# Who fetches which chunk in a three-round graph kernel: SP takes every third unit, ScalarE also works in round one

## The reference

```
ew = (w - min w) / (max w - min w + 1e-8)
h  = relu(layernorm(x))
for each edge:  m = ew * (h[src] @ W1[type]);   h1 = relu(segment_sum(m, dst) + h @ root1 + b1)
for each edge:  m = ew * (h1[src] @ W2[type]);  x  = x + segment_sum(m, dst) + h1 @ root2 + b2
h   = relu(layernorm(x))
out = x + segment_sum(w * h[src], dst) @ W3.T + b3
```

## Time and profile before

| | us |
|---|---|
| median of 3 runs | 5746.92 (5746.85 to 5749.39) |
| profiled execution, its own time | 5746.24 |
| its span | 5744.4 |
| POOL busy | 4320.2 (75%) |
| PE busy | 3123.5 (54%) |
| DVE busy | 1414.0 (25%) |
| ScalarE busy | 439.1 (8%) |

### The profile page before, as it was taken

One profiled execution on the slowest core, in us unless ns is written; L12 is line 12 of the kernel. 1 busy time (PEld: TensorE's weight loads), 2 busy tenths in 40 slices (PEclk: granted clock), 3 DMA queues, 4 the chain that ended last, 5 costly groups with the idle time before them and its releaser, 6 DMA issues.

```text
span 5744.4 us, 66657 instructions
## 1 busy us (share of the span) xinstructions
PE 3123.5 (54%) x11399; PEld 2517.6 (44%) x11399; DVE 1414.0 (25%) x5042; ACT 439.1 (8%) x1183; POOL 4320.2 (75%) x4580
## 2 busy tenths in 40 slices
PE   3766666666666544444444444444444444444444
PEld 3645555545545434434434434434444444444444
DVE  7433333333333222122222222221111111111111
ACT  5111111111111000000000000000000000000000
POOL 7777777777777677777777777777777777777777
PEclk7887877887778655555555555555555555555555
DMA  6222222222222222222222222222222222222222
GB/s 174 82 76 74 72 74 76 72 74 76 72 74 75 63 63 62 61 62 62 61 62 62 62 61 62 62 60 61 62 62 60 62 62 61 62 62 62 61 62 59
DMA packets 291274, 392.97 MB, mean 68 GB/s; under 512 B 94699, under 2 KB 205144, under 8 KB 290840
## 3 DMA queue, kind: packets, MB, share of 16 engines
q0 software_dynamic: 146304, 299.92, 20.0%
q1 hardware_dynamic: 132760, 85.71, 5.0%
q10 hardware_dynamic: 11776, 3.04, 0.2%
HBM read 336.96 MB, written 51.34 MB: 68 GB/s over the span
## 4 chain that ended last, share of the span: by engine, by line
POOL 68%; issue 23%; ACTq 3%; DMA 2%; PE 2%; DVE 1%; ACT 1%; SPq 0%; DVEq 0%; POOLq 0%
POOL rows L558 68%; ACTq L798 2%; DMA rows<-table,idx 2%; ACTq L793 1%; PE bank L975 1%; PE bank L1016 1%; DMA spare_a<-table 0%; ACT acc L628 0%; PE bank L893 0%; PE bank L915 0%; DVE acc L1223 0%; DVE bank L1372 0%; DVE stats L1094 0%; SPq L359 0%; DVE win L1342 0%
## 5 line engine op out<-in xcount | busy, mean ns | idle before, releaser
L558 POOL DMA_INDIRECT rows<-table,idx x4508 | 4254.7, 944 | 1394.8 <-issue 1364.2
L1016 PE MATMUL bank<-win,rows 128*128 128x48 f32 x6064 | 1768.6, 423 | 1837.5 <-DMA rows<-table,idx 1821.9
L1016 PEld LDWEIGHTS bank<-win,rows 128*128 128x128 f32 x6064 | 1458.6, 319 | 2148.1 <-DMA rows<-table,idx 2128.2
L975 PE MATMUL bank<-win,rows 128*128 128x192 f32 x3080 | 856.6, 408 | 638.0 <-DMA rows<-table,idx 493.7
L975 PEld LDWEIGHTS bank<-win,rows 128*128 128x128 f32 x3080 | 596.7, 229 | 849.4 <-DMA rows<-table,idx 672.4
L1223 DVE TENSOR_TENSOR acc<-acc,bank 128x48 f32 x1173 | 239.3, 204 | 1111.2 <-PE bank L893 960.7
L1342 DVE TENSOR_SCALAR win<-iota,key,sw_col 128x192 f32<-128x192 f32 x1563 | 501.4, 391 | 15.9 <-PE bank L908 13.2
L688 ACT ACTIVATE tile_T<-acc 128x128 f32<-128x128 f32 x196 | 60.4, 309 | 2411.2 <-DVE acc L1223 2411.2
L1285 DVE TENSOR_SCALAR idx<-src_col 128x16 int32<-128x16 int32 x98 | 21.6, 223 | 884.8 <-PE bank L1016 884.8
L893 PE MATMUL bank<-sums,W1s 128*128 128x192 f32 (+1 forms) x784 | 219.3, 446 | 0.6 <-ACT sums L736 0.6
L1372 DVE TENSOR_TENSOR bank<-bank,rel 128x384 f32<-128x384 f32 x392 | 218.6, 558 | 0.7 <-issue 0.2
(11 more groups left out here) (123 smaller groups left out, 1311.9 us busy)
## 6 DMA issues: line engine op xcount, KB each, us to landing
spare<-table SPq DMA_DIRECT2D x9088, 0.5 KB
spare_a<-table ACTq DMA_DIRECT2D x5888, 0.5 KB
rows<-table,idx POOLq DMA_INDIRECT x4508, 2.6
table<-st SPq DMA_DIRECT2D x146, 256.0 KB, 2.3
x_rows<-table SPq DMA_DIRECT2D x49, 128.0 KB
x_rows<-in_x_dram SPq DMA_DIRECT2D x48, 128.0 KB
h_rows<-table SPq DMA_DIRECT2D x48, 128.0 KB
out_dram<-st SPq DMA_DIRECT2D x48, 128.0 KB, 2.1
```

The source lines that it names most:

```text
L558: eng.indirect_dma_start(out=rows[:, slot, :], out_offset=None, in_=table[:, :], in_offset=bass.IndirectOffsetOnAxis(ap=idx[:, slot:slot + ...
L975: ins = eng.matmul(half_ps[v % 2 * 2 + h][:, q % 2 * RW:(q % 2 + 1) * RW], chunk_rows(0, u, q * CG + k), wide[:, v % 2, q * CG + k, :], st ...
L1016: ins = eng.matmul(agg_of(u, v, q)[:, q * W:(q + 1) * W], chunk_rows(r, u, q * CG + k), window[:, slot, :], start=(k == 0), stop=(k == n - 1))
```

## The change

`SE` becomes 3: SP fetches chunk 12 of units 5, 8, ... 95 in round 0 and of 2, 5, ... 95 in rounds 1 and 2. A chunk's eight blocks are spread over three passes, as two, three and three. ScalarE fetches chunk 8 (`AK`), the first of a unit's third group, in place of chunk 12, in units 5, 9, ... 93 of rounds 1 and 2 as before, and now also in units 13, 17, ... 93 of round 0 (`AF` = 3: from its fourth on). In round 0 it issues one block at q = 1 and one at q = 3 of each unit, the second ahead of `prep`. A unit can now have both. Another address list is computed on DVE, semaphores are split by round, and one semaphore is dropped from the setup.

```diff
-SE = 4
+SE = 3
 AE = 4
+AF = (3, 1, 1)
...
-    SK = UC - CG
+    SK, AK = UC - CG, UC - 2 * CG
...
-        def by_sp(r, u):
-
-            return u % SE == SE - 1 and (r > 0 or u >= SE)
...
-        def by_act(r, u):
-
-            return r > 0 and u % AE == 1 and AE < u < AO * AE
...
+        def by_sp(r, u, k):
+
+            return k == SK and u % SE == SE - 1 and (r > 0 or u >= RING) and u < NO * SE
+
+        def by_act(r, u, k):
+
+            return k == AK and u % AE == 1 and AF[r] <= u // AE < AO
...
                 else:
-                    j, part = divmod(u + 2, SE)
+                    j, part = divmod(u + 1, SE)
                     if 0 < j < NO:
-                        single_rows(r, j, part * P // SE, (part + 1) * P // SE)
+                        lo, hi = (p * (P // OB) // SE * OB for p in (part, part + 1))
+                        single_rows(r, j, lo, hi)
...
-                    if not is_single(r, u, k):
+                    if not fetched(r, u, k):
                         gather(table, v * UC + k, rows_signal(u, k))
...
+            def act_rows(r, u, lo, hi):
+
+                j, part = divmod(u + AE - 1, AE)
+                if not AF[r] <= j < AO:
+                    return
+                n, b = act_number(r, j), act_buffer(r, j * AE + 1)
+                if part == 0 and lo == 0:
+                    if j == AF[r]:
+                        eng.wait_ge(s_single_at, 8)
+                        for s in range(2):
+                            if r == 0:
+                                eng.wait_ge(s_tabled[s], TABLED[s])
+                            else:
+                                eng.wait_ge(s_stored[s], stored_by(r, s, 0))
...
+                table = in_bytes[r]
+                for e in range(part * P // AE + lo, part * P // AE + hi, OB):
...
                         if q == 2 and u == 1:
                             clear_early()
+                        if q % 2 == 1:
+                            act_rows(0, u, q // 2 * OB, (q // 2 + 1) * OB)
                         if q == UG - 1 and not first(u, 2):
                             eng.wait_ge(s_acc, u * UG)
                             prep(0, u - 2, v % 2)
...
-                    act_rows(r, u)
+                    act_rows(r, u, 0, P // AE)
...
+            eng.tensor_scalar(act_at[0][:, :], act_src[:, :], float(row_bytes), None, ALU.mult).then_inc(s_single_at, 1)
```

More of the change, by code:

```diff
@@ L92, in build @@
         act_src, act_type = sb("act_src", [AO, P], i32), sb("act_type", [AO, P], i32)
-        act_at = [sb(f"act_at{r}", [AO, P], i32) for r in range(2)]
+        act_at = [sb(f"act_at{r}", [AO, P], i32) for r in range(3)]
         single_at = [sb(f"single_at{r}", [NO, P], i32) for r in range(3)]
@@ L138, in build @@
         match_ps = bank[6][:, 64:64 + HC * W].rearrange("p (c w) -> p c w", w=W)
-        s_first, s_first_f, s_first_t = sem("s_first"), sem("s_first_f"), sem("s_first_t")
+        s_first, s_first_t = sem("s_first"), sem("s_first_t")
         s_list = [sem(f"s_list{k}") for k in range(4)]
@@ L163, in build @@
         s_single_list = sem("s_single_list")
-        s_by_act = [sem(f"s_by_act{b}") for b in range(2)]
+        s_by_act = [[sem(f"s_by_act{a}{b}") for b in range(2)] for a in range(2)]
         s_idx_part, s_agg_part = sem("s_idx_part"), sem("s_agg_part")
@@ L231, in rows_signal, with fetched, act_number, act_buffer @@
             return s_tail[k] if u == NU - 1 else s_row[u % RING * UG + k // CG][min(k % CG, CG - 2)]
-        def by_sp(r, u):
-            return u % SE == SE - 1 and (r > 0 or u >= SE)
-        def is_single(r, u, k=SK):
-            return k == SK and (by_sp(r, u) or by_act(r, u))
-        def by_act(r, u):
-            return r > 0 and u % AE == 1 and AE < u < AO * AE
-        def act_number(r, u):
-            return (r - 1) * (AO - 1) + u // AE - 1
+        def by_sp(r, u, k):
+            return k == SK and u % SE == SE - 1 and (r > 0 or u >= RING) and u < NO * SE
+        def by_act(r, u, k):
+            return k == AK and u % AE == 1 and AF[r] <= u // AE < AO
+        def fetched(r, u, k):
+            return by_sp(r, u, k) or by_act(r, u, k)
+        def act_number(r, j):
+            return (0, 0, AO - AF[1])[r] + j - AF[r]
+        def act_buffer(r, u):
+            return ((AO - AF[0] if r else 0) + act_number(r, u // AE)) % 2
         def single_number(r, j):
@@ L255, in single_buffer, with gathers_so_far @@
             return spare[:, n % 2, :]
-        def single_gathers(r, u):
+        def gathers_so_far(r, u, k):
             units_so_far = [(p, w) for p in range(r + 1) for w in range(u % RING, NU - 1 if p < r else u + 1, RING)]
-            return 16 * sum(not is_single(p, w) for p, w in units_so_far)
+            return 16 * sum(not fetched(p, w, k) for p, w in units_so_far)
         def wait_rows(eng, r, u, k):
@@ L265, in wait_rows @@
                 eng.wait_ge(s_tail[k], 16 * (r + 1))
[L266 to L269, removed]
+            elif by_act(r, u, k):
+                eng.wait_ge(s_by_act[r > 0][act_buffer(r, u)], 16 * P * (act_number(r, u // AE) // 2 + 1))
+            elif by_sp(r, u, k):
                 n = single_number(r, u // SE)
@@ L272, in wait_rows @@
                 eng.wait_ge(s_single[r][n % 2], 16 * P * so_far)
-            elif k == SK:
-                eng.wait_ge(rows_signal(u, k), single_gathers(r, u))
+            elif k in (SK, AK):
+                eng.wait_ge(rows_signal(u, k), gathers_so_far(r, u, k))
             elif k % CG < CG - 1:
@@ L281, in chunk_rows @@
         def chunk_rows(r, u, k):
-            if is_single(r, u, k) and by_act(r, u):
-                return spare_a[:, act_number(r, u) % 2, :]
-            if is_single(r, u, k):
+            if by_act(r, u, k):
+                return spare_a[:, act_buffer(r, u), :]
+            if by_sp(r, u, k):
                 return single_buffer(single_number(r, u // SE))
@@ L411, in _ @@
             for to, arr in ((act_src, src), (act_type, etype)):
-                eng.dma_start(to[:, :], arr[0:AO * AE * UC * P].rearrange("(j c e) -> j c e", c=AE * UC, e=P)[:, UC + SK, :]
+                eng.dma_start(to[:, :], arr[0:AO * AE * UC * P].rearrange("(j c e) -> j c e", c=AE * UC, e=P)[:, UC + AK, :]
                               ).then_inc(s_single_list, 16)
@@ L485, in single_rows @@
                     if n == 0:
-                        eng.wait_ge(s_single_at, 7)
+                        eng.wait_ge(s_single_at, 8)
                     elif n > 1:
@@ L730, in finish1_last @@
                     normalise(st[:, h, k * 2 * D:k * 2 * D + D], fin_of(t + k, k)[:, 0:D], 0, k).then_inc(s_fin_a, 1)
+            def act_rows(r, u, lo, hi):
[5 more added lines that the diff above has]
+                    if j == AF[r]:
+                        eng.wait_ge(s_single_at, 8)
+                        for s in range(2):
[3 more added lines that the diff above has]
+                                eng.wait_ge(s_stored[s], stored_by(r, s, 0))
+                    before = [(p, i) for p in range(r + 1) for i in range(AF[p], AO if p < r else j)]
+                    if len(before) > 1:
+                        p, i = before[-2]
+                        if p == 0:
+                            eng.wait_ge(s_half, 2 * (i * AE + 1) + 2)
+                        else:
+                            eng.wait_ge(s_agg, (p - 1) * NU + i * AE + 2)
+                table = in_bytes[r]
+                for e in range(part * P // AE + lo, part * P // AE + hi, OB):
+                    found = nc.values_load_multi_w_load_instructions(
+                        act_at[r][j:j + 1, e:e + OB], engines=(mybir.EngineType.Activation,), min_val=0,
+                        max_val=table.shape[1] - row_bytes,
+                        skip_runtime_bounds_check_because="the lists name nodes of the graph alone")[1]
+                    for k in range(OB):
+                        eng.dma_start(spare_a[e + k:e + k + 1, b, :].bitcast(mybir.dt.uint8),
+                                      table[0:1, bass.ds(found[k], row_bytes)]).then_inc(s_by_act[r > 0][b], 16)
             def first_round():
@@ L775, in first_round @@
                     own_out(t)
[L777 to L799, removed]
             def fast(r):
@@ L850, in _ @@
             eng.wait_ge(s_const, 2)
-            eng.wait_ge(s_first_f, 1)
+            eng.wait_ge(s_first, 17)
             eng.transpose(first_ps[:, 0:P], first_f, ident[:, :]).then_inc(s_first_t, 1)
@@ L1079, in _ @@
             eng.wait_ge(s_first, 16)
-            eng.tensor_copy(first_f, first_f.bitcast(i32)).then_inc(s_first_f, 1)
+            eng.tensor_copy(first_f, first_f.bitcast(i32)).then_inc(s_first, 1)
             link(eng.memset(row0[:, :], 0.0))
@@ L1196, in _ @@
             eng.tensor_scalar(single_at[1][:, :], single_type[:, :], float(row_bytes), None, ALU.mult).then_inc(s_single_at, 1)
[L1197 to L1201, removed]
```

(6 more changed lines are left out.)

## The result

The changed kernel takes 5823.32 us as the median of 4 runs (5822.8 to 5824.81), beside 5746.89 for the kernel before in the same comparison: a ratio of 1.0132, 95% interval 1.0119 to 1.0145. Forecast were 5786 us, 5730 to 5835. The profiled execution took 5822.86 us, its span 5820.9.

What follows compares the result with a forecast made beforehand. POOL's gathers, at a pitch of 1.248 us, were taken as the bound. 5746.2 - 56.2 (gathers saved) + 39.9 (SP's late start) + 56 (ScalarE's late rows) = 5786 us, 8-in-10 range 5730 to 5835.

Steps and rivals of the forecast that it cites:

- Gathers: POOL's table-row gathers, all rounds: 45 fewer at a pitch of 1.248 us, saving 56.2 us.
- SP at the start of round one: SP's late first chunks hold POOL at unit 12 until 290.0 us: one stall of 39.9 us.
- SP later: SP's chunks after its late start, through rounds two and three: no cost, with some 5 us of cover in later rounds.
- ScalarE in round one: ScalarE's two blocks per unit in 84 units delay prep and PE, but cost POOL nothing.
- ScalarE in rounds two and three: ScalarE's late rows, moved to chunk 8, hold POOL: 14 us in round two, 42 in three, 56 us together.
- The forecast's upper bound: For ScalarE's stalls in rounds two and three: 1 us more each, 100 us instead of 56.
- The sum by it, 5809: With 2.0 us fixed DMA cost instead of 1.51, ScalarE's 46 stalls grow up to 0.5 us each, 23 us: 5809.
- A: Rival: only SP's late start costs, ScalarE's moved chunk lands in time: 5730 us, chance 0.10.
- B: Rival: POOL is held neither by SP's late start nor by ScalarE's moved chunk: 5690 us, chance 0.04.
- C: Rival: ScalarE's stalls come but SP's at unit 12 don't: 5746 us, chance 0.04.
- D: Rival: ScalarE's blocks in round one hold PE beyond the cover, 84 units by 1 us: 5870 us, chance 0.07.
- E: Rival: SP, at 97%, falls behind by 1 us in three units, over 27 chunks: 5813 us, chance 0.08.

Runs made afterwards that it cites:

- E2: Changed kernel, but SP's chunks of units 5 and 8 of round one stay with POOL, SP beginning at unit 11: 5786.72 us, ratio 1.0071.
- E6: Changed kernel without ScalarE's chunks in round one: 9109.98 us at a slower pace of issue, ratio 1.144 to the kernel before beside it.
- E1: Changed kernel with ScalarE's four quarters of a chunk issued one unit earlier: 5732.21 us, ratio 0.9973 to the kernel before.
- E4: Changed kernel with places swapped, SP fetching chunk 8 and ScalarE chunk 12: 5737.17 us, ratio 0.9982 to the kernel before.
- E5: Changed kernel with SP's part undone (one chunk every fourth unit, as before), ScalarE's part kept: 5762.75 us, ratio 1.0027 to the kernel before.
- E7: Changed kernel with SP's chunks of rounds two and three left to POOL: 8164.65 us at a slower pace of issue, ratio 1.025; repeated, 1.024.
- E3: Changed kernel, ScalarE's quarters a unit earlier and SP starting at unit 11: 8964.83 us at a slower pace, ratio 1.126; last repetition 8980.14 us.

## Why the prediction came out as it did

**Gathers.** 4463 on table rows and a pitch of 1.248 us: as forecast.

**SP at the start of round one.** As forecast, nearly to the microsecond: unit 11's last row issued at 285.8 (287.6 forecast, with a release at 131.0, not 133.0), POOL held until 288.1 (290.0), 38.6 us in two gaps (39.9), and E2 takes them away. I had not worked out the first gap's share. It is 30 us because PE begins unit 11's third group late too: it stood for unit 8's chunk until 229.93, and then 4.87 and 4.37 us for ScalarE's `prep` at the end of units 9 and 10, in which ScalarE already issues rows. These 9.2 us shift the gaps and don't add to them, since the second gap ends with unit 11's last row whatever the first one was.

**SP later** held by a hair: one excess of 0.3 us at 345.82, where the forecast left 1 us, and none after.

**ScalarE in round one** cost POOL nothing, as forecast: PE waits 55.8 us for prep, 9.2 of them inside SP's stall at unit 12, and no other gap follows. E6, which was to test it, met the other pace.

**ScalarE in rounds two and three** had the right mechanism (E1, E4) and the wrong size: 92.6 us for 56. The rule used, PE's start + 0.66 + 0.26 against 19.98 us after the unit's first gather (18.73 with SP's chunk), gives each stall to 0.1 us when it is fed what the changed trace shows: unit 25, 20.69 + 0.92 - 19.98 = 1.63, measured 1.65. What was mis-sized is PE's start in round two, which the forecast kept at 19.19: it is 19.2 us on average before, 20.4 after, over the 23 units, read off the timelines. The 15 units without SP's chunk, forecast at 0.2 us each, took 1.60; that alone is 21 of the 37 us missed.

| mean us, round two | before | after |
|---|---|---|
| first gather to ScalarE's prep | 4.99 | 5.41 |
| prep to the last issue's end | 12.97 | 13.12 |
| last issue's end to PE's start | 1.24 | 1.89 |

The largest part is the last. In the kernel before that lag was 1.24 us on average over the 23 units of round two, where SP's issues never stood beside ScalarE's last ones, and 2.32 us over the 22 units of round three where they did; in the one where they didn't it was 1.34. The earlier trace rows are one case of each. I had put the difference down to round three as such ("the mean wait is 0.85 longer") and carried 1.24 over to a round two in which SP would issue nearly all the time. After the change, within round two alone, it is 2.57 us in the 8 units with SP issuing at that moment, 1.81 in 8 in which it issued within 4 us of it but not at that moment, and 1.19 in the 7 with none (E2 and E4 show the same split in their round two: 1.35 and 1.32 with none, over 2 us on average otherwise); with SP's old pattern (E5) 1.15 in round two and in round three 2.28, with 1.73 in the one unit where SP was quiet. So the lag goes with SP's issues and not with the round. E7, which was to take them away, met the other pace, so this rests on comparing units and on E5. Other traffic beside the rows, such as SP's stores, was not varied.

The rows themselves hardly moved more slowly. In the packed trace of the kernel before, ScalarE's last packet ended 0.73 us after its last issue in round two and 0.81 in those 22 units of round three; from that packet to the last count of the semaphore that PE waits for it was 0.47 us and 1.48. After the change these are 0.77 and 0.38 in the 7 units of round two without SP, 0.74 and 1.80 in the 8 with it. What grew lies between the packet and the count; why it does isn't shown. The 0.42 us by which PE's end of a unit came later against POOL isn't explained. The forecast's upper bound, 1 us more for each, covered both, and so did its range.

The rule of the Trainium skill on the fixed cost (DMA: Bandwidth & Descriptors, "Anatomy of one DMA — SWDGE (gpsimd) path", about 2.0 us) is written for POOL's path. The lags here, from the last issue's end to PE's start, lie on both sides of it, 1.2 and 2.3 to 2.6 us, so one fixed figure fits neither case. The sum by it, 5809, came nearer than mine, because 2.0 lies near the mean of both rounds after the change, 2.14; the 1.24 us of round two before speak against it.

**Rivals.** A (ScalarE's late rows harmless) is out by the 46 stalls, B (no stall at all) and C (none at unit 12) by the gaps in the trace, D (ScalarE's blocks in round one cost 1 us a unit) and E (SP falls ever further behind) by the absence of any other gap.

## What to carry to other kernels

POOL is the bound here at the first pace, and a fetch that landed late cost time only through the gather that the pacing ties to it. Before a fetch is moved to another place, work out which later instruction waits for that place, and by how much the fetch is late already where it stands. Late rows of ScalarE were free at chunk 12 and cost 92 us at chunk 8, four gathers earlier. A queue that is planned to 97% has no cover for a late start or for slower issue. Issuing ScalarE's quarters a unit sooner made the change pay by 15 us at the first pace (E1). Starting SP two pieces later gave back 37 us by itself (E2), and that both together would add up is not measured.

## What the runs showed that I had not expected

PE could start 1.2 us after ScalarE's last issue without SP's row DMAs beside it and only after 2.3 us with them, while SP's queue, its table loads and stores included, took 5.0% of the DMA engines' time and ScalarE's 0.3%; the extra time lies behind the row's last packet. And the issue of row DMAs from straight-line code isn't a constant of the chip: a chunk of SP with its share of stores took 56 us in the changed kernel's round one (154.8 us from 131.04 to 285.82 for two chunks and three quarters of one) and some 92 in round two of E3's last repetition, on the chip of E1, E2, E4 and E5. In those later runs the kernel before took 37% to 39% longer than at first, and both repairs together were 12.6% to 13.4% slower than it.
